# GpSimd's row gathers and scatters paced by the first layer's products in a routed feed-forward network

## The reference, cut to what matters

```python
weights = (jnp.einsum('bsd,do->bso', x, wr) + br)[..., 0]
_, idx = jax.lax.top_k(weights, k)          # k = 3125
sel_idx = idx[:, :kk]                       # kk = 3124
sel = jnp.take_along_axis(x, sel_idx[:, :, None], axis=1)
h = jax.nn.gelu(jnp.einsum('bkd,dh->bkh', sel, w1) + b1)   # 256 -> 1024
y = jnp.einsum('bkh,hd->bkd', h, w2) + b2                  # 1024 -> 256
y = y * w_sel[..., None]
processed = jnp.zeros_like(x).at[batch_idx, sel_idx].set(y)
return processed + x
```

## Time and profile before

| | us |
|---|---|
| three executions | 2406.88, 2418.86, 2427.03 |
| median | 2418.86 |
| the profiled execution | 2416.03 |
| its span in the profile | 2414.9 |

### The profile page before, as it was taken

The page is one execution under the profiler, slowest core; times in us unless marked ns, Lnnn a source line. Parts: engine busy times, 40 slices in busy tenths (PEclk is TensorE's granted clock), DMA queues, the critical chain, the costliest instruction groups (busy, mean ns, idle before and its releaser), DMA issues.

```text
span 2414.9 us, 37427 instructions
## 1 busy us (share of the span) xinstructions
PE 1963.8 (81%) x10310; PEld 1463.2 (61%) x10310; DVE 1667.4 (69%) x4091; ACT 1465.1 (61%) x4981; POOL 1183.8 (49%) x1207
## 2 busy tenths in 40 slices
PE   5999997995788888888888888888888873835998
PEld 5865554553666666666676666667666652623655
DVE  8957765543678877878887778788788785684111
ACT  6845554563377677777677677677777774651221
POOL 0033334335466656566666565666665641602454
PEclk9999999996899999999999999999999996966999
DMA  5868878897788878788888787888888755681221
GB/s 181 306 232 325 322 309 264 331 391 257 221 264 266 273 247 264 258 267 265 268 278 259 244 273 253 254 266 269 272 277 255 247 177 165 174 281 41 66 71 39
DMA packets 271601, 583.85 MB, mean 242 GB/s; under 512 B 45091, under 2 KB 186100, under 8 KB 264738
## 3 DMA queue, kind: packets, MB, share of 16 engines
q0 software_dynamic: 93936, 384.51, 47.3%
q1 hardware_dynamic: 177458, 196.94, 25.8%
HBM read 407.93 MB, written 176.99 MB: 242 GB/s over the span
## 4 chain that ended last, share of the span: by engine, by line
PE 47%; DVE 21%; issue 11%; another core or an unknown queue 9%; ACT 7%; DVEq 2%; DMA 2%; POOL 0%; SPq 0%; POOLq 0%; ACTq 0%
PE bank L971 9%; PE bank L790 7%; PE bank L955 5%; ACT arena L1337 5%; PE bank L1138 4%; PE bank L769 4%; DVE arena L1951 3%; DVE arena L2044 3%; PE bank L936 2%; DVE arena L2008 2%; PE bank L638 2%; PE bank L851 2%; PE bank L776 2%; PE bank L1127 2%
## 5 line engine op out<-in xcount | busy, mean ns | idle before, releaser
L2343 POOL DMA_INDIRECT arena<-table,arena x880 | 868.6, 987 | 551.2 <-issue 222.0
L1337 ACT ACTIVATE arena<-arena 128x64 f32<-128x64 f32 x3448 | 841.4, 341 | 1.0 <-issue 1.0
L971 PE MATMUL bank<-arena 128*128 128x260 f32 x1760 | 465.3, 402 | 111.5 <-issue 64.0
L971 PEld LDWEIGHTS bank<-arena 128*128 128x128 f32 x1760 | 325.1, 195 | 212.3 <-issue 135.6
L1951 DVE TENSOR_TENSOR arena<-bank,arena 128x512 f32<-128x512 f32 x440 | 302.0, 688 | 205.2 <-remote 156.5
L955 PE MATMUL bank<-arena 128*128 128x256 bf16 x2640 | 343.8, 279 | 16.4 <-issue 14.3
L955 PEld LDWEIGHTS bank<-arena 128*128 128x128 bf16 x2640 | 264.2, 100 | 82.5 <-issue 19.5
L1961 DVE TENSOR_REDUCE arena<-arena 128x16 f32<-128x1024 f32 x220 | 267.8, 1217 | 17.2
L790 PE MATMUL bank<-arena 64*128 64x512 f32 x832 | 210.9, 623 | 24.2 <-DVE arena L1693 18.8
L2044 DVE TENSOR_TENSOR arena<-arena,bank 128x260 f32 x440 | 185.0, 420 | 46.5 <-remote 25.1
L1221 ACT COPY arena<-bank 128x512 f32<-128x512 f32 x260 | 148.9, 595 | 87.7 <-PE bank L790 81.4
(11 more groups left out here) (316 smaller groups left out, 3043.9 us busy)
## 6 DMA issues: line engine op xcount, KB each, us to landing
arena<-q_parts SPq DMA_DIRECT2D x440, 192.0 KB
arena<-chunk_rel SPq DMA_DIRECT2D x220, 128.0 KB
arena<-table,arena POOLq DMA_INDIRECT x880
node_rows<-arena SPq DMA_DIRECT2D x24, 512.0 KB, 6.4
xl_and_sum<-arena SPq DMA_DIRECT2D x3, 3072.0 KB, 18.6
arena<-in_x SPq DMA_DIRECT2D x12, 512.0 KB, 7.7
xn<-arena SPq DMA_DIRECT2D x12, 512.0 KB, 8.6
xT<-arena SPq DMA_DIRECT2D x12, 512.0 KB, 8.3
```

Source lines behind the costliest of these rows:

```text
L971: ins = TE.matmul(bank[b][:, 0:AW], lhsT=so[p % 2][:, c % 2, j, :], rhs=values_of(c, j), start=j == 0, stop=j == HALF - 1)
L1337: ins = A.activation(seg, seg, ACT.Copy, scale=rows[:, C + h:C + h + 1])
L2343: G.indirect_dma_start(rows_of_pair(p, i % 2 * HALF + j), None, d_tab_rows[0:N * R, :], bass.IndirectOffsetOnAxis(ap=idxE[:, g, j, c:c + 1 ...
```

## The change

Four things are done in POOL's queue; nothing is changed on any other engine.

1. The gathers of group g + 1 each wait for one more product of group g's first layer: gather i for product (g, i), i from 0 to 3. Those of group 0 don't wait.
2. Behind the gathers stand four `put_out`, each behind a wait for one more product: (g, 4) to (g, 7).
3. In front of each scatter of y stands one `put_out` instead of two or three.
4. The slots are counted through (`n_put`), so that there are 52 `put_out` as before: 24 + 24 in groups 0 to 5 (four at the products and four at the tiles of each), and the last four at the products 4 to 7 of group 6, none in front of that group's only scatter of y.

```diff
-        def gather_picked(g):
+        def gather_picked(g, spaced):
             if g >= 2:
                 G.wait_ge(y_ready, picked_of(g - 2)[-1] + 1)
             for i, j in enumerate(picked_of(g)):
+                if spaced:
+                    products(g - 1, i)
                 G.indirect_dma_start(pk[g % 2][:, i, :], None, d_pair[:, :],
...
-        gather_picked(0)
+        def products(g, oc):
+
+            b, k = psum.at("f1", g, oc)
+            G.wait_ge(full[b], k)
+
+        gather_picked(0, False)
...
+        n_put = 0
         for g in range(KG):
             if g + 1 < KG:
-                gather_picked(g + 1)
+                gather_picked(g + 1, True)
+            for oc in range(GT, FC):
+                products(g, oc)
+                put_out(n_put)
+                n_put += 1
             for j in picked_of(g):
                 rows = P if j < KT - 1 else KLAST
-                for s in range(j * NTS // KT, (j + 1) * NTS // KT):
-                    put_out(s)
+                if n_put < NTS:
+                    put_out(n_put)
+                    n_put += 1
                 G.wait_ge(y_ready, j + 1)
                 G.indirect_dma_start(out[:, :], bass.IndirectOffsetOnAxis(ap=picked_n[0:rows, j:j + 1], axis=0),
                                      yb[j % NY][0:rows, :], None).then_inc(y_out.sem(j), 16)
+        assert n_put == NTS
```

## The result

Seven executions of the kernel after lie between 2390.43 and 2404.37 us, median 2392.1; the kernel before had 2418.86 (2406.88 to 2428.4, seven executions). The ratio on record is 0.9909, with a 95% interval of 0.9882 to 0.9935: 22 us less of 2419, between 16 and 29. The time was within the range of 2391 to 2424, 1.1 us above its lower end and 10.9 us under the 2403 given, and it is the rival "full relief" that came true.

What follows compares the result with a forecast made beforehand. PE was taken to bound the last network, losing 17.1 us waiting for late GELUs. 17.1 - 5.6 = 11.5, with both clock terms 16.4; 2418.86 - 16.4 = 2402.5, given as 2403, range 2391 to 2424.

Steps and rivals of the forecast that it cites:

- full relief: Rival for the last network: no increment of PE is late; 21.5 us gained, 2397 us, chance 0.17.
- (a): Second layer: two scatters instead of three for a tile, 2.56 us of POOL against 3.84; last y about 0.6 us earlier.
- (b): First layer: gathers wait for products, held by at most a few tenths of a us; 5 us of cover left.
- (c): First layer: four scatters of sums at products 4 to 7, one in 1.74 us; last put can be 2 us late free.
- (d): Group 6: four scatters go nearly back to back (5.1 us) from about 2396.5 as before, without a backlog in front.
- what is left: PE's waits remaining before the second layer: 0.6 us for each of groups 0 to 5, 2.0 in group 6, 5.6 in all.
- The clock terms: Time regained from slow-clock stretches: 1.7 us in group 2's second layer, 3.2 us in the last tile.
- The main forecast: Last network: most late news goes, 5.6 us of waits stay, 16.4 us gained; 2403 us, chance 0.55.
- The reading of the cause: Last network: while POOL issues indirect DMAs back to back, PE's semaphore increments are held up, 2 to 5 us late.
- The slower rival: First layer: each gather waits for a late increment, one every 3.7 us, so PE waits at transposes; 2424 to 2433 us, chance 0.10.
- no relief: Rival: late news comes from DMA number and bytes in flight or is a recording artefact; 2418 us (2412 to 2424), chance 0.18.
- a sentence of the Trainium skill: Says the semaphore write itself is nearly free on this chip; by it, holding gathers back could gain 0.

Runs made afterwards that it cites:

- e2: Kernel after, but the four gathers go without a wait on a product and the scatters keep theirs; ratio 0.9884 to the kernel before.
- e4: Kernel before without any of the 52 scatters of sums; 2399.9 us, the kernel before 2428.2 in the same job.
- e9: Kernel after with each first-layer product made in two halves of 256 columns; 2408.8 us, the kernel before 2429.5 in the same job.
- e12: Kernel after, unchanged, measured once more beside the kernel before; 2408.5 against 2431.4 us, ratio 0.9918.
- e5: Kernel after without waits on products, each first-layer product made in two halves of 256 columns; 2417.4 us, the kernel before 2432.3.
- e6: Kernel before with the second layer made of half as many products of twice the width; 2400.4 us, the kernel before 2432.3.
- e3: Kernel after with the new order of POOL's queue but none of the waits on products; ratio 0.9903 to the kernel before.
- e1: Kernel after without the scatters at products 4 to 7, two or three to a tile again, gathers' waits kept; ratio 0.9944 to the kernel before.
- e10: Kernel after with a wait before each two gathers in the edge stage in place of each four; 2461.0 against 2429.5 us, ratio 1.0115.
- e7: Kernel before with each scatter of sums cut to 64 of its 128 rows; 2433.7 us, the kernel before 2432.3.
- e8: Kernel before with each scatter of sums cut to 64 of its 256 columns; 2403.5 us, the kernel before 2432.3.
- e11: Kernel after with one wait for two pairs in the edge stage, then eight gathers in a row; 2370 us, the kernel before 2194.3, ratio 1.0809.

## Why the prediction was right, and where its steps were off

What bounds the last network was read rightly: PE, and PE's waits for late GELUs. That nothing is added on PE, ACT or DVE, and that no wait of POOL costs anything, held for (a), (b), (c) and (d). The last gather of group 2 went 7.30 us behind the group's first product (2242.06 - 2234.76), where I had expected 7.26 (2246.4 - 2239.14), and PE's transposes never waited for a gather.

The term that was mis-sized is "what is left": 3.6 us in groups 0 to 5 and 2.0 in group 6, 5.6 in all. It measured 2.0, of which 0.8 is the copy of line 1420 in group 5 and 0.7 the GELUs of group 6, with no increment late; e2, e4, e9 and e12 have 1.9 or 2.0 as well. I had taken it from other stages, where POOL issued 0.40 and 0.63 DMAs in a microsecond, as if this rate alone mattered; e5 and e6 show that PE's own instructions count too, so that rates of stages with a different PE can't be carried over. The clock terms, 1.7 and 3.2 us forecast, came to 4.7. With 5.6 put right the gain forecast would have been 16.4 + 3.6 = 20.0; the trace has 19.5.

That the median fell within the range was in part luck. The main forecast (some increments late, 2403, chance 0.55) did not come true; the rival with a chance of 0.17 did, at a price of 21.5 us against 19.5 in the trace. The other 7.3 of the 26.8 us between the medians don't come from the last network. By the medians the kernel is even over 1% faster (2392.1 is under 2394.7), which I had given 0.13; by the ratio, 0.9909, it isn't, and the interval holds both.

The reading of the cause was right in its direction and wrong in a part. "Back to back for long" is not enough: e3 has ten DMAs in a row, with all GELUs in time. The new order, with fewer scatters beside the second layer (part (a)), carries the gain: e3 has it all but for 0.5 us with no wait on a product. How much of it is the y that goes out at once was not told apart. The pacing by products, which gives this text its title, isn't needed: the gathers' waits (b) bring 11.1 us alone (207.1 - 196.0) and nothing that shows beside the new order, as long as PE's first layer isn't denser (e9). The slower rival needed a fourth gather more than 10.5 us into the first layer. In e1, with the backlog still there, the fourth gather of group 2 went 9.6 us into it (2262.64 - 2253.00), not far from that. It failed because POOL had to pause once only, for 2.1 us, and then the backlog was gone.

The rival "no relief" named an artefact of recording as one of its reasons. That the spacing did help doesn't exclude such an artefact, and the last section says what speaks for one. The prediction also counted a sentence of the Trainium skill (DMA: Bandwidth & Descriptors, "Anatomy of one DMA") against its own reading. That sentence is about the increment that a DMA writes at its end; the late ones here are PE's, so this result neither bears it out nor refutes it.

## What to carry to other kernels

When an engine waits and no instruction ended just before, while the producer's work is long done, look at how many DMAs GpSimd issues in that stretch and how dense PE's instructions are there; thin the DMAs out where PE is densest, and bundle them where it is sparse. Writes that nobody waits for are the ones to move. A wait on PE's progress in GpSimd's queue can be a safeguard: here one pause of 2.1 us drained the backlog of a group. It isn't a rule: in the edge stage a finer wait made the kernel 1.2% slower than the kernel before (e10). If the trace has a list of increments, compare it with the ends of the instructions that raise them before building a theory. Before a gain of this kind is taken for good, have the kernel before run again in several jobs: it may exist in one condition only.

## What the runs showed that was not expected

First, that the density of PE's instructions and GpSimd's DMAs make the news late together (e3 against e5: 2.5 and 10.8 us idle; the kernel before against e6: 17.1 and 11.8), while fewer rows or bytes in the scatters don't help (e7, e8).

Second, that the late news can be absent altogether: 2194 us against 2428 for the same kernel, about 235 us or a tenth of its time, and one "remote" wait of 3.4 us in e11's trace. No trace of the kernel before in that condition was kept, so that late news makes up the 235 us is an inference. The traces differ in one more thing: the list of semaphore increments that e11's trace holds has 40869 entries, the ones of all other runs have 17811 to 20739, with about the same instructions and transfers. So late news and lost records go together, in the one trace of this kind. It may be that the recording of increments is overloaded and holds up PE's; that is a guess. It fits that e5 and e6 changed the number of PE's instructions and not that of its increments. Each execution that was timed also came with its recorded span, so none of these runs tells whether the lateness is there without recording. That stays open, as does what sets the condition.

Third, that more waits in POOL's queue made DVE wait longer for late news in the edge stage (e10: 132.1 to 255.6 us at line 1951), though the increments were late by about the same; in the last network waits of the same kind did the opposite.
